# Two expert stages of a two-layer transformer: expert choice inside the stage, match-and-replace, sums by ScalarE, low weight parts by VectorE

## The chip, the cores and the metric

One core of a Trainium2 chip runs the whole program. The metric is the device time of one launch in microseconds (us); lower is better. The median of three launches is given for the kernel before; one further launch was profiled, and all rows of the trace are from that one.

## The reference

Two layers work on x, 2 sequences of 1024 tokens with 128 features (2048 tokens, 16 tiles of 128, 4 chunks of 512). Layer 0 is causal attention (16 heads of 64) and a mixture of 24 packed expert blocks. Layer 1 is a linear attention, and then a block with RMS norm, rotary attention (16 heads of 8), a gate and 8 experts of which each token takes one. What the change touches is, in short:

```python
# layer 0, choice and mixture (E=32, K=4, I=96: 32 x 96 columns are packed as 24 x 128)
scores = sigmoid(x @ gate_w.T)
_, ids = top_k(scores + e_bias, 4)
w = take(scores, ids); w = w / sum(w)
combine = zeros(T, 32).at[tokens, ids].add(w)
out = einsum(silu(x @ w1) * (x @ w3) * combine, w2)
# layer 1: RMS norm ahead of q, k, v
h = ln1_w * x * rsqrt(mean(x * x) + 1e-6)
# layer 1, choice and mixture (E=8, K=1, 256 hidden)
top1 = argmax(h2 @ Wr + br)
u1, u2 = split(h2 @ W1 + b1)
y = (u1 * sigmoid(u2)) @ W2 + b2, of expert top1 alone
```

## The kernel before

The program is a row of stages, each a block in which the five engines run their own lists and after which they meet at a barrier. In order: `stage_load`; `stage_ln` n0; `stage_attention64` a0; n1; `stage_combine` c0; `stage_experts` e0; n2; `stage_linear`; n3; `stage_rope`; `stage_attention8` a1; `stage_gate`; c1; e1; `stage_finish`. Every DMA is issued by SyncE (SP), so there is one queue.

**The choice** (`stage_combine`, L1108 to L1184) works on the logits of all 16 tiles. For layer 0 ScalarE takes the sigmoid (L1129) and VectorE adds the bias (L1144). VectorE finds each tile's eight largest (L1146), asks for their places (L1149), casts the places (L1151), compares them one rank at a time with a ramp 0..31 (L1155) and adds the masks (L1158); it multiplies by the scores, sums, inverts and scales (L1160 to L1163). TensorE transposes the 16 tiles (L1173), VectorE copies them out (L1167), and SP stores the table to DRAM (L1183; three copies for e0, since 32 experts of 96 columns lie in 24 blocks of 128). Layer 1 takes one expert, without scores.

**The experts** (`stage_experts`, L1187 to L1432). Values and weights are each split in a high part, rounded to the fast matmul format, and a low part, the rest; a product is three matmuls. A job is one chunk of 512 tokens with one 128-wide column block: e0 has 24 experts of 4 jobs, e1 8 experts of 8 jobs. For each job TensorE does six up matmuls (L1286) into two banks; ScalarE applies silu or sigmoid to one (L1359, L1361) and VectorE multiplies (L1416, L1418), which frees the banks; VectorE multiplies by the expert's row of the choice table (L1423), ScalarE rounds the product (L1339), VectorE takes the low part (L1397), and TensorE does three down matmuls (L1298) that accumulate in banks 4 to 7. TensorE runs two jobs ahead in the up part. On VectorE the order within job i is L1416 of job i, L1397 of job i-1, L1423 of job i.

The next expert's weights are rounded by ScalarE at its job 1 (L1329, up) and job 3 (L1333, down), and GpSimd subtracts to get the low parts (L1379). SP's order per expert is: wait until the low parts two experts earlier are taken; load the up weights (L1247, L1248) and down weights (L1251); wait until the expert before last is through (`f_full`); load the expert's rows of the table, broadcast over the partitions, as four DMAs of 256 KB (L1255). e1 has one DMA of 1 MB there, and starts with four bias matmuls that multiply the 8-row table (L1305).

**The norm with RMS** (`stage_ln` n3): TensorE transposes the centred tiles back (L192), ScalarE scales them out (L306) and squares them (L310), TensorE sums the squares by a matmul with a column of ones (L208) beside each tile's projection (L210), ScalarE takes the root of the four sums (L316), VectorE inverts (L263) and scales the tile (L1959).

## Time and profile before

| | |
|---|---|
| median of three launches | 1588.23 us (1587.38 to 1591.88) |
| profiled execution, whole | 1587.51 us |
| profiled execution, span of the trace | 1585.8 us |
| TensorE (PE) busy | 1323.0 us, 83% |
| VectorE (DVE) busy | 1019.7 us, 64% |
| ScalarE (ACT) busy | 666.4 us, 42% |
| GpSimd (POOL) busy | 206.5 us, 13% |
| mean granted TensorE clock | 0.893 |

In the rows, times count from the span's start; "idle before <-releaser" is how long the engine had stood still and what ended that. A group of several instructions stands as one row with its count (x4), and its second number is then the time from the first start to the last end. PEld are weight loads, SPq is the DMA issue on SyncE. A granted clock of 1.00 is 2.4 GHz, 0.50 is 1.2 GHz.

### The profile page before, as it was taken

To read this page: it belongs to the slowest core of one execution; us is meant where nothing else is said; L and a number is where in the kernel's file an instruction comes from. 1 tells how busy PE (TensorE), PEld (TensorE's weight loads), DVE (VectorE), ACT (ScalarE), POOL (GpSimd) and SP (SyncE) were. 2 spreads that over 40 slices of the span, in tenths; PEclk is the share of its full clock that TensorE was granted. 3 is DMA by queue.
4 is the path that set the end of the run, shared out by engine and by line. 5 is a ranking of instruction groups with operands and counts; after the bars stand their busy time and mean duration, and the time that the engine had idled before them with its cause. 6 is when DMAs were issued, how large, how long until landed. Compare 5 with 4: busy or idle time off the path is not lost. (4 is left out here: it accounts for less than half of the span.)

```text
span 1585.8 us, 19829 instructions
## 1 busy us (share of the span) xinstructions
PE 1323.0 (83%) x6224; PEld 806.0 (51%) x6224; DVE 1019.7 (64%) x1731; ACT 666.4 (42%) x1222; POOL 206.5 (13%) x417
## 2 busy tenths in 40 slices
PE   4789999999999999546999987614898988579997
PEld 3345555555655555234777765512343443146886
DVE  4645556475746462266999985564777875057998
ACT  2133434334243423134555555221366666215664
POOL 0001111111111111001111100031011111003110
PEclk9689999999999999768999998555799999568998
DMA  3110202111120201106676720034032211103220
GB/s 86 32 36 6 54 10 54 37 26 42 21 63 0 62 0 31 31 1 140 137 151 132 152 63 1 0 98 115 1 72 55 53 46 28 52 2 120 74 99 27
DMA packets 42833, 87.67 MB, mean 55 GB/s; under 512 B 13601, under 2 KB 31657, under 8 KB 37545
## 3 DMA queue, kind: packets, MB, share of 16 engines
q1 hardware_dynamic: 42768, 86.86, 23.0%
q8 instruction: 35, 0.57, 0.2%
q14 instruction: 30, 0.24, 0.0%
HBM read 69.47 MB, written 8.45 MB: 49 GB/s over the span
## 5 line engine op out<-in xcount | busy, mean ns | idle before, releaser
L646 ACT ACTIVATE shared<-ps 128x1024 f32<-128x1024 f32 (+7 forms) x256 | 165.9, 651 | 358.6 <-PE ps L495 358.0
L510 PE MATMUL ps<-shared,Vg 128*65 128x512 f32 (+3 forms) x768 | 291.1, 487 | 10.8 <-POOL shared L677 8.5
L1286 PE MATMUL ps<-qA 128*128 128x512 f32 x960 | 254.5, 401 | 19.2 <-DVE qA L1403 12.9
L561 DVE TENSOR_REDUCE mraw<-ps 128x1 f32<-128x512 f32 (+3 forms) x304 | 195.9, 659 | 89.4 <-PE ps L462 61.3
L964 DVE TENSOR_REDUCE mraw<-ps 128x2 f32<-128x1024 f32 (+3 forms) x160 | 174.0, 1114 | 76.5 <-PE ps L884 57.6
L1286 PEld LDWEIGHTS ps<-qA 128*128 128x128 f32 x960 | 178.3, 191 | 76.7 <-DVE shared L1416 18.1
L1008 ACT ACTIVATE shared<-ps 128x512 f32<-128x512 f32 (+2 forms) x320 | 154.2, 563 | 127.0 <-PE ps L900 126.8
L493 PE MATMUL ps<-qA,kH 128*128 128x512 f32 (+3 forms) x384 | 168.2, 446 | 2.6 <-DMA qB<-mT 2.6
L456 PE MATMUL ps<-kH,qA 128*128 128x512 f32 (+3 forms) x384 | 162.7, 464 | 6.2 <-DVE mraw L561 2.8
L510 PEld LDWEIGHTS ps<-shared,Vg 128*65 128x65 f32 x768 | 98.4, 138 | 118.4 <-issue 83.5
L1339 ACT CAST qA<-shared 128x512 fp32r<-128x512 f32 x160 | 99.3, 621 | 134.9 <-DVE shared L1423 134.5
L677 POOL TENSOR_SCALAR_AFFINE_SELECT shared<-shared 128x128 f32<-128x128 f32 x256 | 81.0, 317 | 526.4 <-ACT shared L646 526.4
L1298 PE MATMUL ps<-qA,kH 128*128 128x512 f32 x480 | 136.0, 392 | 4.3 <-DVE qA L1397 4.3
L495 PE MATMUL ps<-qB,kL 65*128 65x512 f32 (+3 forms) x384 | 134.4, 350 | 0.0
L1423 DVE TENSOR_TENSOR shared<-shared 128x512 f32<-128x512 f32 x160 | 132.3, 827 | 0.1
L1397 DVE TENSOR_TENSOR qA<-shared,qA 128x512 fp32r<-128x512 f32 x160 | 112.3, 702 | 10.9 <-ACT qA L1339 1.4
L1298 PEld LDWEIGHTS ps<-qA,kH 128*128 128x128 f32 x480 | 89.6, 188 | 25.5 <-DVE qA L1397 6.6
L456 PEld LDWEIGHTS ps<-kH,qA 128*128 128x128 f32 x384 | 72.4, 201 | 53.1 <-DVE mraw L561 30.3
L873 PE MATMUL ps<-kL,qA 64*128 64x512 f32 (+3 forms) x288 | 65.7, 436 | 36.1 <-DMA kH<-k_split 30.3
L900 PE MATMUL ps<-qA,kH 64*128 64x512 f32 (+3 forms) x288 | 81.5, 446 | 12.9 <-ACT shared L1008 8.1
L917 PE MATMUL ps<-shared,VP 128*32 128x512 f32 (+3 forms) x768 | 88.3, 536 | 0.5 <-ACT oU L996 0.5
L493 PEld LDWEIGHTS ps<-qA,kH 128*128 128x128 f32 x384 | 74.3, 193 | 27.3 <-issue 16.9
(227 smaller groups left out, 1595.9 us busy)
## 6 DMA issues: line engine op xcount, KB each, us to landing
shared<-comb SPq DMA_DIRECT2D x96, 256.0 KB, 4.5
qB<-qA SPq DMA_DIRECT2D x8, 1024.0 KB, 7.0
rB<-a0rec_dram SPq DMA_DIRECT2D x8, 1024.0 KB, 7.2
shared<-comb SPq DMA_DIRECT2D x8, 1024.0 KB, 4.4
q_split<-qA SPq DMA_DIRECT2D x8, 512.0 KB
qA<-q_split SPq DMA_DIRECT2D x16, 256.0 KB, 4.4
rB<-a1rec_dram SPq DMA_DIRECT2D x32, 128.0 KB, 2.7
e0wUp<-in_w SPq DMA_DIRECT2D x48, 64.0 KB, 4.6
```

Of the source, the lines that this page charges most:

```text
L456: ins = nc.tensor.matmul(bank[:, j * width:(j + 1) * width], k.qA[par][:, h0 + j, qt * P:(qt + 1) * P], k.kH[par][:, ch * 512:ch * 512 + w ...
L493: nc.tensor.matmul(region[:, lo:hi], kH[:, kt * P:(kt + 1) * P], qA[:, h, lo:hi], start=True, stop=False)
L495: ins = nc.tensor.matmul(region[:, lo:hi], kL[0:hd + 1, kt * P:(kt + 1) * P], qB[0:hd + 1, h, lo:hi], start=False, stop=True)
L510: ins = nc.tensor.matmul(O[0:65, lo:hi], k.Vg[par][:, kt, :], k.PT[:, slot % PTR, lo:hi], start=(kt == 0), stop=(kt == 4 * ch + 3))
L561: ins = nc.vector.tensor_reduce(out, bank[:, 0:n_h * width].rearrange("p (h w) -> p h w", w=width), AX, ALU.max)
L646: nc.scalar.activation(k.PT[:, slot % PTR, kt * P:S], score_banks(slot)[:, kt * P:S], ACT.Exp, scale=scale).then_inc(p_full, 1)
L964: nc.vector.tensor_reduce(out[:, :, js[0]:js[-1] + 1, qt % 4], src, AX, ALU.max).then_inc(x_free, 1)
L1008: nc.scalar.activation(dst, src, ACT.Exp, scale=scale).then_inc(p_done, 1)
L1286: ins = nc.tensor.matmul(bank[0:M, :], w[par][:, at:at + M], h[:, cols], start=(r == 0), stop=(r == 2))
L1298: ins = nc.tensor.matmul(acc(ch), w[par][:, m * D:(m + 1) * D], f[0:M, i % 2, :], start=(opens and r == 0), stop=(closing and r == 2), ski ...
L1397: nc.vector.tensor_tensor(fL[0:M, i % 2, :], k.hid[0:M, i % 2, :], fH[0:M, i % 2, :].bitcast(F32), ALU.subtract).then_inc(a_full, 1)
L1423: nc.vector.tensor_tensor(k.hid[0:M, i % 2, :], mul, k.cb[0:M, par, ch * 512:(ch + 1) * 512], ALU.mult).then_inc(f_full, 1)
```

## The change

It has six parts, and nothing else moves.

1. `stage_combine` is gone; its work stands at the head of `stage_experts`, so that weight loads, the splitting of values and weights, and the first up job run in the same block as the choice.
2. The choice uses match-and-replace: the unwanted ranks of the eight largest are overwritten, the tile's matching values are replaced by a mark, and a comparison with the mark gives the mask.
3. The rows of expert 0 come from a matmul of the table with a constant 0/1 matrix (`k.sel`) and not from DRAM. e0 reads them in PSUM, e1 has them copied by ScalarE.
4. The low parts of the weights are made by VectorE (GpSimd keeps those of expert 0), and ScalarE rounds the next up weights at job 0 and not at job 1.
5. In n3 the outputs are transposed once more, and ScalarE squares and sums in one instruction per tile; the matmuls with ones are gone.
6. The first two q/k weight loads of a0 are issued in `stage_load`.

```diff
+                for group in range(2):
+                    sp.dma_start(k.wqk[:, group, :], a["wqk0"][0]).then_inc(k.a0_in[group], 16)
                 for dst, src in later:
...
                 if rms:
-                    pe.wait_ge(squared, ch + 1)
+                    for t in range(4 * ch, 4 * ch + 4):
+                        ins = nc.tensor.transpose(k.bank(4 + ch)[:, (t % 4) * P:(t % 4 + 1) * P],
+                                                  dst[:, t * P:(t + 1) * P], k.ident[:, :])
+                    ins.then_inc(squared, 1)
...
-                    if rms:
-                        nc.tensor.matmul(k.bank(t % 4)[:, width:width + 1], sq[:, t * P:(t + 1) * P],
-                                         k.one_col[:, :], start=True, stop=True)
...
+                for t in range(4 * ch, 4 * ch + 4):
+                    ins = nc.scalar.activation(sq[:, t * P:(t + 1) * P], k.bank(4 + ch)[:, (t % 4) * P:(t % 4 + 1) * P],
+                                               ACT.Square, accum_out=k.rms_sum[:, t:t + 1])
+                ins.then_inc(summed, 1)
...
# stage_experts, SP
-                load(0, 0)
+                sp.wait_ge(copied, NC)
+                for r in range(copies):
+                    sp.dma_start(rows[:, r, :], k.cT[0:CE, :]).then_inc(stored, 16)
+                sp.wait_ge(stored, 16 * copies)
                 load(1, 1)
...
# TensorE
+                up(0, 0, 0)
+                pe.wait_ge(weights, 1)
+                for t in range(NT):
+                    ins = nc.tensor.transpose(acc(t // 4)[0:CE, (t % 4) * P:(t % 4 + 1) * P], comb[:, t, :],
+                                              k.ident[:, :])
+                for ch in range(NC):
+                    if ch == 1:
+                        up(0, 0, 1)
+                    pe.wait_ge(copied, ch + 1)
+                    nc.tensor.matmul(acc(ch), k.sel[0:CE, choose.sel, :], k.cT[0:CE, ch * 512:(ch + 1) * 512],
+                                     start=True, stop=True, skip_group_check=True).then_inc(rows_full, 1)
...
# ScalarE, per expert
-                        if i == 1 and not last:
+                        if i == 0 and not last:
                             split(e + 1, 1 - par, half + par)
...
# GpSimd
+                low(0, wL[0], wUp[:, 0, :], wH[0])
+                low(1, dL[0], wD[0:M, 0, :], dH[0])
-                with pool.Fori(0, E // 2) as j:
-                    for par in range(2):
-                        low(4 * j + 2 * par, wL[par], wUp[:, par, :], wH[par])
-                        low(4 * j + 2 * par + 1, dL[par], wD[0:M, par, :], dH[par])
...
# VectorE
+                low_part(0)
+                if choose.gated:
+                    link(nc.vector.tensor_tensor(logits[:, :, :], score[:, :, :],
+                                                 choose.e_bias.unsqueeze(1).broadcast_to((P, NT, CE)), ALU.add))
+                for t in range(NT):
+                    ins = nc.vector.max(top[:, t, :], logits[:, t, :])
+                link(nc.vector.memset(top[:, :, choose.K:8], ABSENT))
+                for t in range(NT):
+                    ins = nc.vector.match_replace(comb[:, t, :], top[:, t, :], logits[:, t, :], CHOSEN)
+                if choose.gated:
+                    link(nc.vector.scalar_tensor_tensor(out=comb[:, :, :], in0=comb[:, :, :], scalar=CHOSEN,
+                                                        in1=score[:, :, :], op0=ALU.is_equal, op1=ALU.mult))
+                    link(nc.vector.tensor_reduce(tot[:, 0, :], comb[:, :, :], AX, ALU.add))
+                    link(nc.vector.reciprocal(tot[:, 1, :], tot[:, 0, :]))
+                    nc.vector.tensor_tensor(comb[:, :, :], comb[:, :, :], column(tot[:, 1, :], NT, CE), ALU.mult)\
+                        .then_inc(weights, 1)
+                for ch in range(NC):
+                    if ch + 1 < NC:
+                        low_part(ch + 1)
+                    dve.wait_ge(turned, ch + 1)
+                    nc.vector.tensor_copy(k.cT[0:CE, ch * 512:(ch + 1) * 512], acc(ch)[0:CE, :]).then_inc(copied, 1)
...
+                        if i == 0 and not last:
+                            low_weights(2 * e + 2, wL[1 - par], wUp[:, 1 - par, :], wH[1 - par])
+                        if i == 3 and not last:
+                            low_weights(2 * e + 3, dL[1 - par], wD[0:M, 1 - par, :], dH[1 - par])
```

VectorE at job 0 of expert 1 in e0, up to the first step of job 1; `shared` holds the gate, the product and the rows of the table, `ps` the banks, `qA` the split parts. Before:

```order
L1416 TENSOR_TENSOR shared<-ps,shared 128x512 [waits e0s_full,e0ld1]
L1397 TENSOR_TENSOR qA<-shared,qA 128x512 [waits e0f_high]
L1423 TENSOR_TENSOR shared<-shared 128x512 [waits e0up_free]
L1416 TENSOR_TENSOR shared<-ps,shared 128x512 [waits e0s_full]
L1397 TENSOR_TENSOR qA<-shared,qA 128x512 [waits e0f_high]
```

Now, with the lines of the changed kernel (L1353 is the old L1397, L1429 the old L1423, L1373 the low parts of the weights):

```order
L1416 TENSOR_TENSOR shared<-ps,shared 128x512 [waits e0s_full,e0ld1]
L1353 TENSOR_TENSOR qA<-shared,qA 128x512 [waits e0f_high]
L1429 TENSOR_TENSOR shared<-shared 128x512 [waits e0up_free]
L1373 TENSOR_TENSOR qA<-e0wUp,qA 128x256 [waits e0w_high]
L1416 TENSOR_TENSOR shared<-ps,shared 128x512 [waits e0s_full]
L1353 TENSOR_TENSOR qA<-shared,qA 128x512 [waits e0f_high]
```

One instruction more stands behind the last step of job 0, and one (128x128) behind that of job 3.

TensorE at the head of the first expert stage. Before, in two blocks:

```order
L1173 MATMUL ps<-ident,c0comb 32x128 [waits c0weights]
L1173 MATMUL ps<-ident,c0comb 32x128 x15
L1125 UNCONDITIONAL_BRANCH
L1274 UNCONDITIONAL_BRANCH [waits barrier_Pool_Activation_PE_DVE_SP_release]
L1286 MATMUL ps<-qA 128x512 [waits e0up_free,e0w_low,e0h_low]
L1286 MATMUL ps<-qA 128x512 x5
L1286 MATMUL ps<-qA 128x512 [waits e0up_free]
```

Now, in one (L1227 the up matmuls, L1247 the transposes of the table, L1255 the 0/1 matmuls):

```order
L1227 MATMUL ps<-qA 128x512 [waits e0up_free,e0h_low,e0w_low]
L1227 MATMUL ps<-qA 128x512 x5
L1247 MATMUL ps<-ident,oU 32x128 [waits e0weights]
L1247 MATMUL ps<-ident,oU 32x128 x15
L1255 MATMUL ps<-y,sel 128x512 [waits e0copied]
L1227 MATMUL ps<-qA 128x512 [waits e0up_free,e0h_low]
L1227 MATMUL ps<-qA 128x512 x5
L1255 MATMUL ps<-y,sel 128x512 [waits e0copied] x3
```

The first up job now runs ahead of the transposes, and four fp32 matmuls over 512 columns are new.

## Rows read from the trace of the kernel before

**Rows 1.** Timeline, layer 0 from norm n1 to expert 1: start, duration, engine, line, out<-in.
```profile
699.12 1.59 DVE L1146 MAX8 c0top<-logits 128x8 f32<-128x32 f32 x16
...
703.44 0.23 DVE L1151 CAST c0atf<-c0at 128x128 f32<-128x128 uint32 x1
...
711.48 3.60 PE L1173 MATMUL ps<-ident,c0comb 128*32 128x128 f32 x16 [15.56 <-DVE c0pick L1164]
...
715.82 1.45 SPq L1183 DMA_DIRECT2D comb<-y  x3
721.36 0.36 SPq L1247 DMA_DIRECT2D e0wUp<-in_w  x1
...
739.96 0.68 DVE L1416 TENSOR_TENSOR shared<-ps,shared 128x512 f32<-128x512 f32 x1
```

**Rows 2.** Timeline, e0, end of one expert and the next one's start.
```profile
774.29 0.68 DVE L1423 TENSOR_TENSOR shared<-shared 128x512 f32<-128x512 f32 x1
...
775.00 0.62 ACT L1339 CAST qA<-shared 128x512 fp32r<-128x512 f32 x1 [0.86 <-DVE shared L1423]
...
775.65 0.69 DVE L1397 TENSOR_TENSOR qA<-shared,qA 128x512 fp32r<-128x512 f32 x1
...
776.18 0.77 POOL L1379 TENSOR_TENSOR qA<-e0wUp,qA 128x256 fp32r<-128x256 f32 x1 [3.74 <-ACT qA L1329]
776.26 1.23 DVE L1423 TENSOR_TENSOR shared<-shared 128x512 f32<-128x512 f32 x1
...
777.71 0.38 SPq L1248 DMA_DIRECT2D e0wUp<-in_w  x1
...
782.29 0.59 ACT L1359 ACTIVATE shared<-ps 128x512 f32<-128x512 f32 x1
```

**Rows 3.** Timeline, e0, VectorE's first step of the last expert.
```profile
932.10 0.68 DVE L1416 TENSOR_TENSOR shared<-ps,shared 128x512 f32<-128x512 f32 x1
```

**Rows 4.** Up weights of two experts, issue to landing, windows 777.2:778.1 and 786.2:787.1.
```profile
DMA to landing us min/median/max: 4.9/5.0/5.0
...
DMA to landing us min/median/max: 4.3/4.4/4.5
```

**Rows 5.** Groups by shape, VectorE, a 128x128 tensor_tensor.
```profile
L1155 DVE TENSOR_TENSOR c1comb<-iota,c1atf 128x128 f32<-128x128 f32 x1 | 0.3, 291 | 0.0
```

**Rows 6.** Timeline, e1, last experts, TensorE not held up.
```profile
1554.62 1.52 PE L1286 MATMUL ps<-qA 128*128 128x512 f32 x6
...
1562.78 1.52 PE L1286 MATMUL ps<-qA 128*128 128x512 f32 x6
```

**Rows 7.** Timeline, e1, the same ScalarE step four experts apart.
```profile
1474.61 0.62 ACT L1329 CAST qA<-e1wUp 128x512 fp32r<-128x512 f32 x1
...
1541.47 0.62 ACT L1329 CAST qA<-e1wUp 128x512 fp32r<-128x512 f32 x1
```

**Rows 8.** Timeline, norm n3: transposes back (chunks 2 and 3), two ScalarE tiles, last scaling.
```profile
1010.65 1.09 PE L192 MATMUL ps<-ident,oU 128*128 128x128 f32 x4 [1.40 <-ACT oU L298]
...
1016.20 0.87 ACT L298 ACTIVATE oU<-x_res,ln_nb,ln_rs 128x128 f32<-128x128 f32 x2
...
1017.21 1.09 PE L192 MATMUL ps<-ident,oU 128*128 128x128 f32 x4 [1.21 <-ACT oU L298]
...
1028.84 1.39 DVE L1959 SCALAR_TENSOR_TENSOR shared<-ps,rms_r,rows 128x192 f32<-128x192 f32 x4
```

**Rows 9.** Timeline, c1 and head of e1: search, bias matmuls, third up job.
```profile
1415.57 1.19 DVE L1146 MAX8 c1top<-logits 128x8 f32<-128x8 f32 x16 [0.30 <-PEq L1679]
...
1427.09 7.16 PE L1305 MATMUL ps<-y,b 8*128 8x512 f32 x8 [3.61 <-PEq L1125]
...
1441.20 1.66 PE L1286 MATMUL ps<-qA 128*128 128x512 f32 x6 [1.26 <-DVE shared L1418]
```

**Rows 10.** Windows, head of e1: PE, PEld, DVE, ACT, POOL busy, PEclk, DMA.
```profile
1430.00:1433.00 3.00, 3.00 (x4) 1.11 (x4) 1.81 (x3) 2.71 (x6) 3.00 (x3) 0.50 0.95 295
```

**Rows 11.** Timeline, head of a0.
```profile
42.01 5.54 PE L446 MATMUL ps<-hT,wqk 128*128 128x512 f32 x8 [3.25 <-DMA wqk<-in_wqk]
```

More of the change, by code:

```diff
@@ L30 @@
 MASKED = -1e30
+ABSENT = -3e38
+CHOSEN = 3e38
 LN_EPS, RMS_EPS = 1e-5, 1e-6
@@ L1211, in stage_experts @@
         JOBS = NC * MT
-        parts = comb_dram.shape[0] // E
+        parts = 4 if choose.gated else 1
         NLD = 16 * (parts + (bias is not None))
+        CE, logits = choose.E, choose.logits
+        scored, weights, turned, copied, stored, rows_full, rows_taken, links = (
+            sem(n) for n in ("scored", "weights", "turned", "copied", "stored", "rows_full", "rows_taken", "links"))
+        score, comb = (k.oU_flat[:, i * NT * CE:(i + 1) * NT * CE].rearrange("p (t e) -> p t e", t=NT)
+                       for i in range(2))
+        top = sb("top", [P, NT, 8])
+        tot = sb("tot", [P, 2, NT])
         UP = 2 * MT * M
@@ L1263, in _ @@
                     load_down(e, e)
-                load(0, 0)
+                if bias is not None:
+                    sp.dma_start(bi[:, 0, :], one(bias, 0)).then_inc(ld[0], 16)
+                sp.wait_ge(copied, NC)
+                copies = comb_dram.shape[0] // CE
+                rows = comb_dram.rearrange("(e r) t -> e r t", r=copies)
+                for r in range(copies):
+                    sp.dma_start(rows[:, r, :], k.cT[0:CE, :]).then_inc(stored, 16)
+                sp.wait_ge(stored, 16 * copies)
                 load(1, 1)
@@ L1345, in _ @@
                     nc.scalar.copy(hH[:, cols], hT[:, cols]).then_inc(h_high, 1)
+                    if ch == 0 and choose.gated:
+                        nc.scalar.activation(score[:, :, :], logits[:, :, :], ACT.Sigmoid).then_inc(scored, 1)
+                    if ch == 0:
+                        split(0, 0, 0)
+                        split_down(0, 0, 0)
+                if MT > 1:
+                    for ch in range(NC):
+                        act.wait_ge(rows_full, ch + 1)
+                        nc.scalar.copy(k.cb[:, 0, ch * 512:(ch + 1) * 512], acc(ch)).then_inc(rows_taken, 1)
                 def expert(e, par, half, first=False, last=False):
                     if bias is not None:
-                        act.wait_ge(ld[par], NLD * (half + 1))
+                        act.wait_ge(ld[par], NLD * (half + 1) if par else NLD * half + 16)
                     for i in range(JOBS):
@@ L1406, in expert @@
+                for ch in range(NC):
+                    if ch + 1 < NC:
+                        low_part(ch + 1)
+                    dve.wait_ge(turned, ch + 1)
+                    nc.vector.tensor_copy(k.cT[0:CE, ch * 512:(ch + 1) * 512], acc(ch)[0:CE, :]).then_inc(copied, 1)
                 def expert(e, par, half, first=False, last=False):
-                    dve.wait_ge(ld[par], NLD * (half + 1))
+                    if not first:
+                        dve.wait_ge(ld[par], NLD * (half + 1) if par else NLD * half + 16 * (bias is not None))
+                    elif bias is not None:
+                        dve.wait_ge(ld[0], 16)
```

163 lines of the change are left out of this document (58 added, 105 removed).

## The prediction

> **What bounds the kernel now.** The busy shares (TensorE 83%, VectorE 64%) are means over fifteen stages, so I read the timeline of each stage that the change touches, then the windows for the granted clock, and last the landing times of the weight loads. The attention stages are left alone but for one load.
>
> At the head of e0 TensorE stands still for long stretches, since choice, table, loads and splitting come one after the other: VectorE starts the search at 699.12, the transposes start at 711.48, the stores at 715.82, the first weight load only at 721.36, and expert 1 starts on VectorE at 739.96 [rows 1].
>
> Inside e0 a ring of VectorE and ScalarE sets the pace, not a sum of busy times. L1423 starts at 774.29; its result is rounded by ScalarE from 775.00 for 0.62; L1397 starts at 775.65 and the next L1423 at 776.26 [rows 2]. That is 1.97 us per job. VectorE has three steps in it that follow each other at 0.61 (775.65 to 776.26), so 0.14 is free. Where GpSimd makes low parts at the same time, L1423 takes 1.23 and not 0.68 [rows 2]. Over experts 1 to 22 the period is (932.10 - 739.96) / 22 = 8.73 us [rows 1, 3], against 4 x 1.97 = 7.88 for the bare ring. So GpSimd's company costs 0.85 per expert. TensorE, where nothing holds it up, needs (1562.78 - 1554.62) / 4 = 2.04 us per job [rows 6], 8.16 per expert. It is the next floor.
>
> **The change, part by part**, against the profiled execution (1587.51 us; its span is 1585.8, so 1.7 lie around it, and it is 0.7 below the median of the three runs).
>
> *First loads of a0.* TensorE waits 3.25 us for them [rows 11]. With them issued in the first stage the wait goes. What is left is the start of the block, some tenths. Gain 2.0 to 3.2, taken **2.5**.
>
> *Head of e0, data path.* The new search starts about 0.6 after the old one, since VectorE takes a low part first: 699.7. Sixteen searches take 1.6 [rows 1], to 701.3. A memset and sixteen match-and-replace follow: the nearest rows are the sixteen index finds, from 700.7 to 703.44, 2.7 us [rows 1]; the bounds are 1.6 (one instruction each, as the search) and 4. That gives 704.1. Four steps then stand for twelve: mask times score, sum, scale at 0.7 each and a reciprocal, 2.5 in all: 706.6, against 711.48 before. Transposes 3.6 [rows 1]: 710.2. Four copies of 0.68 alternate with low parts of 0.6, so the last ends at 711.6. The stores take 721.36 - 715.82 = 5.5 from first issue to next load, a little less without the barrier, 5.2: 716.8. Then come the rows and weights of the next experts. In steady state the second up load is issued at 777.71, which is 2.74 after L1423 ended at 774.97, and lands 4.4 to 5.0 later [rows 2, 4], so 7.1 to 7.7 after the burst begins, taken 7.5: 724.3. Rounding those weights and the first gate cost 1.0, since both now stand ahead of expert 1's first step: 725.3, against 739.96. Gain 14.7.
>
> *Head of e0, TensorE's path.* The 0/1 matmuls are fp32 over 512 columns, as the bias matmuls of e1, of which four chunks took 7.16 at 1.2 GHz [rows 9, 10]; between half of that and the whole. The up job before the second of them costs 1.4 to 2.6. From 710.2, all at 1.2 GHz, job 2's matmuls would end at 722.3 and expert 1 start at 727.0: gain 13. At 2.4 GHz the data path decides. I take **14**, with 12 to 15.5 as bounds.
>
> *Steady e0.* GpSimd's 0.85 goes. VectorE takes the low parts instead: 128x256 and 128x128. A 128x128 one lasts 0.29 [rows 5], 512 wide 0.69, so 256 wide 0.42 between them. Followers overlap by 0.08, so they occupy 0.34 and 0.21. Less the 0.14 that is free each time, the ring grows to 7.88 + 0.20 + 0.07 = 8.15, level with TensorE's 8.16. But the up weights are now rounded at job 0 instead of job 1, **ahead of a gate that the ring needs**. The load is issued behind the 1 MB of rows and lands 7.1 to 7.7 after the expert before last ended. Rounding 256 columns delays the gate by some 0.3 (512 take 0.62 [rows 2]), and ScalarE starts 0.05 after a landing. The gate takes 0.59 [rows 2], and L1416 may come 0.12 after the end of the last L1423, behind the new low part, which starts 0.08 before that end and occupies 0.2; so the gate must start 0.5 before that end if the ring is to stay whole. The period is at least 7.1 to 7.7 plus 0.3 + 0.05 + 0.5, or 7.95 to 8.55, and over TensorE's 8.16 on average 8.37. Before, the rounding came one job later and found the weights there. Gain (8.73 - 8.37) x 22 = **8**, between 0 and 12.5. GpSimd's own work is not needed elsewhere in that stage. SP's wait for low parts is met earlier than its wait for `f_full`, so its loads move with the experts and no further.
>
> *n3.* One cycle is 1017.21 - 1010.65 = 6.56, the tail 1028.84 + 1.39 - 1017.21 = 13.0 [rows 8]. TensorE loses the matmuls with ones and gains four transposes per chunk (1.09, rows 8). The important part is that ScalarE no longer waits for the projections before it takes the root and then the next centring. The new squares are unseen in this trace: between 0.2 and 0.65 each, the nearest row being two tiles of 128x128 in 0.87 [rows 8], taken 0.4. A cycle is then a transpose back and a transpose (2.1), four squares (1.6), the root and centring (1.3): 5.0. Over one and a half cycles and a shorter tail the gain is 3.5 to 8.8, taken **5.5**.
>
> *Head of e1.* The block now starts with the search, at 1415.6 [rows 9]. Load, rounding and GpSimd's low part take some 4.7 (2.7, 0.6 and 1.4, as estimates), so the first up job ends near 1422.9, and the transposes, 3.6 as in e0 [rows 1], near 1426.5. There the bias matmuls could start, 0.6 before now; but the four 0/1 matmuls (3.6 to 7.2) and the second up job (1.4 to 2.6) now stand ahead of them. The bias matmuls ran from 1427.09 for 7.16 us without a gap, and the granted clock in 1430 to 1433 was still 0.50, 1.2 GHz [rows 9, 10]. Eight-row matmuls do not raise it here. All at 1.2 GHz the third up job ends at 1426.5 + 7.2 + 2.6 + 7.2 + 2.6 = 1446, against 1442.9 now [rows 9]; with the up jobs at 2.4 GHz near 1441; all at 2.4 GHz near 1436.5. Gain -3 to +6.5, taken **2**. The Trainium skill, page "TensorE: Matmul & The Clock Gate", Part 1, says that "the default state is throttled, and activity releases the throttle". Read plainly, a TensorE that is busy throughout would run this head at the high level, for a gain of 6.5. The trace speaks against it for eight-row matmuls.
>
> *Steady e1.* The period is (1541.47 - 1474.61) / 4 = 16.72 [rows 7]. Ring 8 x 1.98, plus low parts of twice the width less the free time, 0.69: 16.53, over TensorE's 16.32. Gain 0.19 x 7 = **1.3**, between 0 and 2.8.
>
> Sum: 2.5 + 14 + 8 + 5.5 + 2 + 1.3 = 33.3. 1587.5 - 33.3 = **1554 us**.
>
> **Rivals.**
> A. *The weights land in time anyway.* The two landings differ by 0.6 [rows 4], and at the early end the period is 8.16, so e0 gains 12.6 and the time is 1549.5. The late landing speaks against it. Chance 0.25.
> B. *The steady part gives nothing*: each expert waits 0.4 longer than forecast for weights, and the period stays 8.73. 1562. Chance 0.17.
> C. *The clock is high in both heads.* e1 gains 6.5 and e0 15: 1549. The clock in rows 10 speaks against it. By the page's rule above this would be the course. Chance 0.10.
> D. *Slower: ScalarE's early rounding turns every expert into a DMA round trip.* ScalarE's queue holds gate and rounding of the product behind the wait, so every microsecond of a late landing is one of the ring. The other terms give 25.3. To be slower by 0.3% the period must reach 8.73 + (25.3 + 4.8) / 22 = 10.1, a landing 9.3 after the burst begins. At 10.2 the time is 1594.5. For it: the 1 MB stands ahead of the weights in SP's queue. Against: the landings seen are 7.1 to 7.7. Chance 0.05, of which 0.02 end within 0.3%.
>
> **How the numbers follow.** The forecast has 0.43, A 0.25, B 0.17, C 0.10, D 0.05. A measurement of this kernel can tell about 0.3% (4.8 us) from no change. All but D are faster by more: faster 0.95, same 0.02, slower 0.03. The low end takes A and C together with a good n3 (1554 - 4.6 - 5 - 3 = 1541), the high end B with a head of e1 at 1.2 GHz and little from n3 (1554 + 8 + 5 + 1 = 1568).
>
> **What would show it.** Right: the first up load issued within 1 us of the stage's start; stores some 4 us earlier than before; expert 1 of e0 starting 14 us earlier after the last logits; L1429 at 0.68 throughout; an e0 period near 8.4 with ScalarE's L1281 waiting for the DMA of `wUp`; TensorE idle before the third up job of e1. Wrong: a period of 8.16 with no such wait (A) or 8.7 (B); a granted clock of 1.00 during the bias matmuls (C); n3 cycles still over 6 us, if a square with its sum costs more than 0.65.

## The result

| | before | changed |
|---|---|---|
| median, us | 1588.93 (1587.38 to 1591.88, 4 runs) | 1547.91 (1539.19 to 1555.47, 4 runs) |
| ratio, 95% interval | | 0.9737 (0.9694 to 0.978) |
| profiled execution, its span | 1587.51, 1585.8 | 1549.17, 1547.5 |

The kernel is 2.6% faster, 41 us by the medians; 1554 was forecast, with 1541 to 1568 as the range. I divide the 38.3 us between the two profiled executions by steps that both traces have. The last column is the same changed kernel profiled once more (experiment 9); its gains sum to 48.1.

| stretch | before | changed | gain | forecast | gain, second profile |
|---|---|---|---|---|---|
| start to the last logits of e0 | 696.15 | 694.24 | 1.9 | 2.5 | 1.9 |
| to expert 1 of e0 (its first step on VectorE) | 43.81 | 32.56 | 11.25 | 14 | 14.3 |
| expert 1 to 23 of e0 | 192.14 | 181.49 | 10.65 | 8 | 11.3 |
| to the first step of n3 | 62.18 | 64.08 | -1.9 | 0 | -0.9 |
| n3 | 35.95 | 24.14 | 11.8 | 5.5 | 11.6 |
| attention and gate of layer 1 (unchanged) | 385.04 | 385.67 | -0.6 | 0 | 4.8 |
| gate's end to expert 1 of e1 | 41.86 | 38.95 | 2.9 | 2 | 2.8 |
| expert 1 to 7 of e1 | 100.30 | 99.18 | 1.1 | 1.1 | 1.1 |
| expert 7 to the end | 28.37 | 27.19 | 1.2 | 0.2 | 1.2 |

### The profile after

Timeline of the head of e0, which answers to [rows 1]. L1179 is a load of up weights, L1381 the search, L1392 the last step of the choice, L1247 the table's transposes, L1202 the stores, L1255 the 0/1 matmuls, L1187 the rows of expert 1, L1227 the up matmuls, L1416 VectorE's first step of a job.

```profile
694.51 0.33 SPq L1179 DMA_DIRECT2D e0wUp<-in_w  x1
...
697.85 1.59 DVE L1381 MAX8 e0top<-logits 128x8 f32<-128x32 f32 x16
...
704.10 0.69 DVE L1392 TENSOR_TENSOR oU<-oU,e0tot 128x512 f32<-128x512 f32 x1
...
704.85 3.59 PE L1247 MATMUL ps<-ident,oU 128*32 128x128 f32 x16 [3.47 <-DVE oU L1392]
708.37 2.07 PE L1255 MATMUL ps<-y,sel 32*128 32x512 f32 x2
...
709.62 1.45 SPq L1202 DMA_DIRECT2D comb<-y  x3
710.37 2.93 PE L1227 MATMUL ps<-qA 128*128 128x512 f32 x6
713.23 5.49 PE L1255 MATMUL ps<-y,sel 32*128 32x512 f32 x6
...
714.77 1.72 SPq L1187 DMA_DIRECT2D shared<-comb  x4
...
718.65 5.05 PE L1227 MATMUL ps<-qA 128*128 128x512 f32 x12
...
726.80 0.69 DVE L1416 TENSOR_TENSOR shared<-ps,shared 128x512 f32<-128x512 f32 x1
```

From 704.85 on TensorE has no gap up to expert 1: it is the engine that the head waits for. The windows (busy times, then the granted clock, where 1.00 is 2.4 GHz) say at which level it ran:

```profile
698.00:715.00 17.00, 13.08 (x32) 7.19 (x33) 13.47 (x65) 4.78 (x8) 0.82 (x2) 0.50 0.23 50
715.00:727.00 12.00, 12.00 (x33) 7.70 (x32) 5.12 (x10) 3.68 (x8) 0.00 (x0) 0.66 0.50 105
```

Inside e0: groups from 727 to 908 (busy, mean ns, idle before and its cause), and one expert's end in the timeline, which answers to [rows 2].

```profile
L1429 DVE TENSOR_TENSOR shared<-shared 128x512 f32<-128x512 f32 x88 | 60.1, 683 | 0.0
...
L1281 ACT CAST qA<-e0wUp 128x256 fp32r<-128x256 f32 x21 | 8.5, 407 | 12.3 <-DMA e0wUp<-in_w 12.3
```

```profile
776.29 1.87 SPq L1187 DMA_DIRECT2D shared<-comb  x4
...
783.55 0.68 DVE L1429 TENSOR_TENSOR shared<-shared 128x512 f32<-128x512 f32 x1
783.75 0.41 ACT L1281 CAST qA<-e0wUp 128x256 fp32r<-128x256 f32 x1 [0.84 <-DMA e0wUp<-in_w]
784.07 0.59 ACT L1318 ACTIVATE shared<-ps 128x512 f32<-128x512 f32 x1
...
784.69 0.69 DVE L1416 TENSOR_TENSOR shared<-ps,shared 128x512 f32<-128x512 f32 x1 [0.25 <-ACT shared L1318]
...
908.29 0.68 DVE L1416 TENSOR_TENSOR shared<-ps,shared 128x512 f32<-128x512 f32 x1
```

L1429 (the old L1423) takes 0.68 to 0.69 everywhere. ScalarE's rounding, which waited for the weights, starts 7.46 us after SP's burst of loads began (776.29 to 783.75), inside the forecast's 7.1 to 7.7. ScalarE's gate starts 0.32 later, and VectorE waits 0.25 for it. The mean period is (908.29 - 726.80) / 22 = 8.25, against 8.73 in [rows 1, 3].

Timeline of n3, which answers to [rows 8]: L196 turns back, L208 are the new transposes, L214 the projections, L317 the squares with the reading of their sum. The first row is from the kernel before: ScalarE's root, which waited 2.83 us for TensorE's projections; the squares now wait 1.25 for the transposes alone.

```profile
1016.04 0.26 ACT L316 ACTIVATE rms_std<-ps,eps 128x4 f32<-128x4 f32 x1 [2.83 <-PE ps L210]
```

```profile
985.57 0.77 PE L196 MATMUL ps<-ident,oU 128*128 128x128 f32 x4
...
986.17 0.60 PE L208 MATMUL ps<-ident,hT 128*128 128x128 f32 x4
...
986.61 1.47 PE L214 MATMUL ps<-ffn_w,hT 128*128 128x192 f32 x8
987.05 0.27 ACT L317 ACTIVATE rB<-ps 128x128 f32<-128x128 f32 x1
987.21 0.20 ACT L317 ACTIVATION_READ_ACCUMULATOR rB<-ps 128x1 f32 x1
987.30 0.27 ACT L317 ACTIVATE rB<-ps 128x128 f32<-128x128 f32 x1
...
989.43 0.63 PE L196 MATMUL ps<-ident,oU 128*128 128x128 f32 x4 [1.35 <-ACT oU L302]
...
990.53 0.28 ACT L317 ACTIVATE rB<-ps 128x128 f32<-128x128 f32 x1 [1.25 <-PE ps L208]
...
995.12 1.39 DVE L1975 SCALAR_TENSOR_TENSOR shared<-ps,rms_r,rows 128x192 f32<-128x192 f32 x4
```

This cycle is 3.86 (985.57 to 989.43) against 6.56, and the tail from the last turn back 7.1 against 13.0. From about 986 on TensorE runs at the high level (granted clock 0.96 from 985 to 997): four transposes take 0.60 to 0.63, against 1.09 in [rows 8]. The cycle before it still ran at the low level (0.50 from 981 to 985, transposes of 1.08 and 1.06) and took 4.55, so most of the shorter cycle was there without the high clock.

Timeline of the head of e1, which answers to [rows 9]:

```profile
1392.75 1.12 PE L1255 MATMUL ps<-y,sel 8*128 8x512 f32 x2
...
1395.39 2.84 PE L1255 MATMUL ps<-y,sel 8*128 8x512 f32 x6
...
1398.07 6.22 PE L1260 MATMUL ps<-y,b 8*128 8x512 f32 x8
```

The first 0/1 matmul takes 1.12 for its two records, where the first one of e0 took 2.07, and the other three take 2.84; the granted clock from 1390 to 1398 is 0.87. The bias matmuls (L1260) took 6.22, 0.9 less than in [rows 9].

### The profile page after: what moved, and what is told of

It reads as the page before. It is cut to its first block and busy times, and to the rows that moved or that the text cites. A ratio compares the mean times of both kernels' runs of the same rounds, so it can differ in the third digit from the quotient of the medians.

```text
span 1547.5 us, 19708 instructions
## 1 busy us (share of the span) xinstructions
PE 1316.2 (85%) x6224; PEld 806.3 (52%) x6224; DVE 1002.8 (65%) x1782; ACT 678.9 (44%) x1254; POOL 157.7 (10%) x357
## 5 line engine op out<-in xcount | busy, mean ns | idle before, releaser
L516 PE MATMUL ps<-shared,Vg 128*65 128x512 f32 (+3 forms) x768 | 291.0, 487 | 11.3 <-POOL shared L683 8.5
L1227 PE MATMUL ps<-qA 128*128 128x512 f32 x960 | 254.3, 402 | 10.1 <-POOL qA L1337 10.1
L1227 PEld LDWEIGHTS ps<-qA 128*128 128x128 f32 x960 | 183.1, 194 | 60.6 <-POOL qA L1337 11.8
L1291 ACT CAST qA<-shared 128x512 fp32r<-128x512 f32 x160 | 99.2, 620 | 90.9 <-DVE shared L1429 90.1
L1353 DVE TENSOR_TENSOR qA<-shared,qA 128x512 fp32r<-128x512 f32 x160 | 109.9, 687 | 6.4 <-ACT qA L1291 1.4
L1429 DVE TENSOR_TENSOR shared<-shared 128x512 f32<-128x512 f32 x156 | 106.6, 683 | 0.0
```

Source lines behind the costliest of these rows:

```text
L516: ins = nc.tensor.matmul(O[0:65, lo:hi], k.Vg[par][:, kt, :], k.PT[:, slot % PTR, lo:hi], start=(kt == 0), stop=(kt == 4 * ch + 3))
L1227: ins = nc.tensor.matmul(bank[0:M, :], w[par][:, at:at + M], h[:, cols], start=(r == 0), stop=(r == 2))
L1353: nc.vector.tensor_tensor(fL[0:M, i % 2, :], k.hid[0:M, i % 2, :], fH[0:M, i % 2, :].bitcast(F32), ALU.subtract).then_inc(a_full, 1)
L1429: nc.vector.tensor_tensor(k.hid[0:M, i % 2, :], mul, rows, ALU.mult).then_inc(f_full, 1)
```

## The experiments

The edits are to the kernel before (1, 2, 6, 11) or to the changed one. Spans of stretches are those of the table. Ratios are to runs of the kernel before on the same chip.

**1. `b_n3`: the kernel before with the new n3 alone.** The edit is the diff of the change in `stage_ln`, with the sums kept in `k.rms_r` until the reciprocals take their place.

> The kernel before with the new n3 alone (squares with their sums by ScalarE, over transposes back). The trace of the changed kernel says that n3 gave 11.8 us, not the 5.5 forecast. Theory 1 (n3 stands by itself): from the first step of n3 on VectorE to the end of the last scaling 24 to 25 us against 35.95 before, transposes back 3.9 us apart, and a time of 1588.9 - 11.8 = 1577 us. Theory 2 (part of what n3 showed came from the state in which the earlier stages left TensorE's clock or from other parts): n3 takes 28 to 31 us and the time is near 1583. Both: L208's transposes let TensorE's projections run at the higher clock, 1.5 us for eight and not 2.8.

Measured: 1579.97 us, ratio 0.9942 (0.9913 to 0.997), 9.2 us less. The first and last VectorE steps of n3:

```profile
995.97 0.32 DVE L270 TENSOR_SCALAR ffn_w<-ffn_w,cols 128x192 f32<-128x192 f32 x1 [0.31 <-PEq L1454]
...
1018.78 1.39 DVE L1961 SCALAR_TENSOR_TENSOR shared<-ps,rms_r,rows 128x192 f32<-128x192 f32 x4
```

n3 takes 24.2 us and stands by itself: theory 1. The gain of the whole kernel, 4.8 to 13.8 by the interval, is compatible with 11.8.

**2. `b_turns`: more transposes in the old n3.**

```
                 if rms:
+                    for t in range(4 * ch, 4 * ch + 4):
+                        nc.tensor.transpose(k.bank(4 + ch)[...], dst[...], k.ident[:, :])
                     pe.wait_ge(squared, ch + 1)
```

> The kernel before, with four transposes per chunk more on TensorE in n3, whose results nobody uses; squares and sums stay as they were. If the higher granted clock is what made n3 short (the transposes keep TensorE busy, the projections then run at 2.4 GHz), n3 shrinks from 35.95 to 30 to 33 us though TensorE has more to do. If it is the chain (ScalarE no longer waits for projections before root and next centring), n3 grows to 37 to 40 us here, 0.5 to 1.1 us per chunk for the transposes, with cycles of 6.5 to 7.5 us.

Measured: 1599.01, one run; n3 takes 38.05, 2.1 more than before. The turns back of chunks 2 and 3:

```profile
1015.90 1.09 PE L192 MATMUL ps<-ident,oU 128*128 128x128 f32 x4 [1.40 <-ACT oU L301]
...
1023.32 1.09 PE L192 MATMUL ps<-ident,oU 128*128 128x128 f32 x4 [1.21 <-ACT oU L301]
```

The cycle grows from 6.56 to 7.42 and the clock stays at 0.50 from 1009 to 1036. More work for TensorE is not what shortened n3, and did not bring the high clock; the chain is the theory left.

**3. `a_pool`: low parts of the weights by GpSimd again,** rounding left at job 0.

```
...
+                with pool.Fori(1, E // 2) as j:
+                    for par in range(2):
+                        low(4 * j + 2 * par, wL[par], wUp[:, par, :], wH[par])
+                        low(4 * j + 2 * par + 1, dL[par], wD[0:M, par, :], dH[par])
...
-                        if i == 0 and not last:
-                            low_weights(2 * e + 2, wL[1 - par], wUp[:, 1 - par, :], wH[1 - par])
...
```

> The changed kernel with the low parts of the weights made by GpSimd again, from expert 1 on; the rounding stays at job 0. If GpSimd's company is what cost 0.85 per expert (L1429 at 1.23 us where both run), the period of e0 grows from 8.25 to 8.7 to 9.0 us and the time by 10 to 16 us over the changed kernel, so 1558 to 1564. If the landing of the weights sets the period now, GpSimd's part overlaps with slack: the period stays within 8.25 to 8.35 and the time within 1546 to 1550.

Measured: 1546.44, ratio 0.971 (0.9653 to 0.9767), experts 1 to 23 of e0 in 179.8, a period of 8.17. The first theory falls as it was put: GpSimd's company costs nothing here. The second, that GpSimd's part overlaps with slack, is nearer, but 8.17 lies below its 8.25 to 8.35. In e1, experts 1 to 7 take 97.4, against 99.2 in the changed kernel: there GpSimd's low parts are the cheaper ones. Timeline of one low part:

```profile
780.89 0.81 POOL L1337 TENSOR_TENSOR qA<-e0wUp,qA 128x256 fp32r<-128x256 f32 x1 [1.50 <-ACT qA L1281]
...
781.34 0.69 DVE L1422 TENSOR_TENSOR shared<-ps,shared 128x512 f32<-128x512 f32 x1 [0.25 <-ACT shared L1318]
```

The VectorE step that starts inside GpSimd's span is one with an operand in PSUM, and keeps its 0.69. From 745 to 900 that is so 38 times, at 0.69 on average. In the trace of before it was the product with the rows, both operands in SBUF, in all 36 cases of the same window, at 1.09 on average (0.95 or 1.23, as in [rows 2]). The Trainium skill, page "SBUF — State Buffer", section "SBUF: two separate sides", says the same: a VectorE instruction "in a 2-port perf mode, or with two SBUF inputs" and a GpSimd one that reads SBUF exclude each other, and the one that starts second waits. By that rule, the trace agrees.

**4. `a_split1`: rounding and low part of the up weights back at job 1,** still by VectorE.

```
-                        if i == 0 and not last:
+                        if i == 1 and not last:
                             split(e + 1, 1 - par, half + par)
...
```

> The changed kernel with the rounding of the next up weights (and their low part) back at job 1. If the wait of ScalarE's L1281 for the weights is what keeps the period at 8.25 and not 8.16, it goes: no idle before L1281 for the DMA in e0, period 8.16 to 8.18, 2 us less over 22 experts, about 1546. If the order of steps around the low part costs instead, the period stays at 8.25 or grows to 8.4 since TensorE waits for the low part of the weights at the next expert's first job.

Measured: 1545.57, ratio 0.971 (0.9655 to 0.9765). The period is (903.23 - 723.52) / 22 = 8.17, TensorE's 8.16 in nearly every expert, and the wait for the DMA is gone. Group of L1281, 727 to 908:

```profile
L1281 ACT CAST qA<-e0wUp 128x256 fp32r<-128x256 f32 x21 | 8.5, 407 | 11.7 <-PE ps L1227 11.7
```

So the early rounding costs the changed kernel 0.08 per expert, 1.8 us in all (0.05 against the second profile, experiment 9): the forecast's mechanism, at less than half its size (8.37 - 8.16 = 0.21).

**5. `a_order`: SP asks for weights ahead of rows.**

```
...
+                        load_weights(2 * j + par + 1, 1 - par)
                         sp.wait_ge(f_full, JOBS * (2 * j + par - 1))
                         load(2 * j + par, par)
...
```

> The changed kernel with SP's queue in another order: the weights of expert e+1 are asked for ahead of the 1 MB of rows of expert e, not behind it. If ScalarE's wait at job 0 is for weights that queue behind the rows, it goes: no idle before L1281 for the DMA, period of e0 8.16, gain 2 us (1546). If it is the landing time by itself, or if rows now come late for VectorE's L1429, the period is 8.25 or more.

Measured: 1547.86, ratio 0.9784 (0.9741 to 0.9827). The wait for weights went, and another came: the period is 8.43. Group of VectorE's first step of a job, 727 to 900:

```profile
L1424 DVE TENSOR_TENSOR shared<-ps,shared 128x512 f32<-128x512 f32 x83 | 56.9, 686 | 5.8 <-DMA shared<-comb 5.6 <-issue 0.2
```

The rows, now last in the queue, come late for VectorE. Whichever of the two loads is asked for last comes late for its first user. Experiment 4 moved that user by a job for the weights; nothing of the kind was tried for the rows.

**6. `b_split0`: the kernel before with the rounding at job 0.** One line, `i == 1` to `i == 0`.

> The kernel before with one thing changed: ScalarE rounds the next expert's up weights at job 0, not job 1, so GpSimd's low part of them starts elsewhere against VectorE's steps. The run with GpSimd's low parts in the changed kernel had L1429 at 0.69 throughout, and GpSimd beside a step that reads PSUM. Theory 1 (the 0.55 came only because GpSimd's work began just ahead of a VectorE step with both operands in SBUF): the period of e0 falls from 8.73 to 8.16 to 8.3, L1423 at 1.23 goes, about 10 us less: 1578. Theory 2 (GpSimd's company costs the ring whatever its moment; in the other run something else, the shorter queue or the table's place, made room): period 8.6 to 8.8 and no change of time.

Measured: 1581.24, ratio 0.9965 (0.9931 to 0.9998). Experts 1 to 23 of e0 take 183.8 (8.36 each) and not 192.1; L1423 is at 1.23 in 2 experts and not in 22, but the down weights' low part still meets it at 0.95, 23 times. Theory 1, at 8.3 us and not 10, and with a period just above its 8.16 to 8.3. The line also acts in e1, which the expectation left out: experts 1 to 7 take 97.4 and not 100.3, 2.9 less. Against that, expert 1 starts 1.4 later in e0 and 1.3 later in e1. One line of the change gives four fifths of what e0's steady part gained, and in e1 more than the changed kernel (1.1); 5.6 us arrive in the kernel's time (0.3 to 11).

**7. `a_warm`: unused transposes at the heads,** on top of the edit of 5.

```
...
+                keep_busy(13)
                 up(0, 0, 0)
+                keep_busy(12)
                 pe.wait_ge(weights, 1)
```

> As the run before, with 13 transposes of 128x128 whose results nobody uses ahead of the first up job and 12 behind it in both expert stages, in time in which TensorE stands still. Theory 1 (the heads are long because TensorE starts them at 1.2 GHz out of idle time): the transposes of the table, 3.6 us now, and the 0/1 matmuls, 0.85 to 1 each now, run at 2.4 GHz (1.9 in all and 0.48 each); expert 1 of e0 starts 24 to 28 us after the last logits and not 32.8; 5 to 9 us less in all, about 1540. Theory 2 (narrow matmuls with 32 or 8 rows keep or bring the lower clock whatever went before): the table's transposes may be short, but the 0/1 and bias matmuls are at 1.2 GHz again; gain 0 to 3 us.

Measured: 1546.89, ratio 0.9747 (0.9704 to 0.9789). The head of e0, TensorE (L1254 the unused ones, L1262 the table's, L1270 the 0/1 matmuls):

```profile
699.17 1.86 PE L1254 MATMUL ps<-ident,hT 128*128 128x128 f32 x12
702.83 1.92 PE L1262 MATMUL ps<-ident,oU 128*32 128x128 f32 x16 [1.81 <-DVE oU L1407]
704.68 1.12 PE L1270 MATMUL ps<-y,sel 32*128 32x512 f32 x2
...
707.33 2.84 PE L1270 MATMUL ps<-y,sel 32*128 32x512 f32 x6
```

All narrow matmuls of this head run faster: 1.92 for 3.59, and 1.12 + 2.84 for 2.07 + 5.49. Expert 1 starts 26.9 us after the last logits, 2.6 sooner than in experiment 5 (29.5), to which this run adds the transposes. Of the 5.6 us to the changed kernel's 32.6, 3.1 are there without them. Theory 1 holds for the matmuls that it names: from 702 to 710 the granted clock is 1.00, so matmuls of 32 rows run at the high level when TensorE comes to them busy. But behind them it fell again, though TensorE had no gap:

```profile
710.20:713.60 3.40, 3.40 (x8) 2.67 (x9) 0.41 (x1) 0.60 (x2) 0.00 (x0) 0.50 0.53 116
```

`a_again` has the same: 1.00 from 714 to 716, under the 0/1 matmuls, and 0.50 from 717 to 720, behind them. So theory 2 is not out; whether the narrow matmuls bring the clock down is not shown, since no run fills their place with wide ones. In e1 nothing came (39.7 from the gate's end to expert 1, against 38.95). In the whole kernel it can't be told from experiment 5, whose interval overlaps with this one's.

**8. `a_rowsdma`: rows of expert 0 of e0 by DMA as before,** its four 0/1 matmuls left out.

```
+                if MT == 1:
+                    load(0, 0)
                 load(1, 1)
```

> The changed kernel, where in e0 the rows of expert 0 come by DMA from the stored table as before, and the four 0/1 matmuls of e0 are gone (e1 is left as it is). If those matmuls are what held the head (7.6 us of them at 1.2 GHz on TensorE's path), the rows land about 5 us after their issue, at 720 where L1429 took the matmul's at 711, but expert 1 starts only 0 to 3 us later than in the changed kernel. If the DMA round trip is what the 0/1 matmuls save, expert 1 starts 5 to 8 us later (732 to 735 on the same scale).

Measured: 1554.18, one run; expert 1 starts 35.6 us after the last logits, 3.1 later than in the profile of the changed kernel and 6.1 later than in its repeat. VectorE stood still for 11.7 us until the rows had landed, and TensorE as long:

```profile
719.75 0.69 DVE L1432 TENSOR_TENSOR shared<-shared 128x512 f32<-128x512 f32 x1 [11.71 <-DMA shared<-comb]
```

The 0/1 matmuls are worth 3 to 6 us, by the level that they meet; neither theory's numbers alone.

**9. `a_again`: the changed kernel, nothing altered.**

> The changed kernel once more, with nothing altered. Its times lie between 1539 and 1555 us and the profiles of its variants disagree on stages that no variant touches: from the end of n3 to the end of the last gate 380.5 to 396.8 us. Theory 1 (the granted clock of TensorE differs from one execution to the next at the same instructions): expert 1 of e0 starts either 29.4 or 32.6 us after the last logits with the same instructions, n3 24.1 to 24.7, e0 from expert 1 to 23 again 181 to 182, and the stretch without changes anywhere in 378 to 397. Theory 2 (the first profile is typical, the differences come from the edits): 32.6, 181.5 and 385.7 again, within 0.5.

Measured: 1540.66 (1532.31 to 1548.86, 4 runs), ratio 0.9677 (0.9606 to 0.9749). The same instructions as in the timeline above, from the table's 0/1 matmuls on:

```profile
713.26 2.92 PE L1255 MATMUL ps<-y,sel 32*128 32x512 f32 x6
...
723.81 0.69 DVE L1416 TENSOR_TENSOR shared<-ps,shared 128x512 f32<-128x512 f32 x1
```

Expert 1 starts 29.55 us after the last logits and not 32.56: L1255 takes 2.92 for 5.49. `a_split1`, `a_pool` and `a_order` also have 29.3 to 29.6, and `a_ones`, whose edit lies in n3, has 32.0. The unchanged stretch took 380.25. Over all profiles of this study it took 378.5 to 396.8. Windows of it, first of `b_n3` (378.5 in all), then of `a_pool` (396.8):

```profile
1220.00:1320.00 100.00, 88.58 (x784) 39.94 (x776) 76.36 (x82) 66.33 (x139) 15.86 (x26) 1.00 0.19 45
1320.00:1398.70 78.70, 53.59 (x297) 25.66 (x289) 22.11 (x40) 30.83 (x61) 6.97 (x11) 0.78 0.11 32
```

```profile
1190.00:1290.00 100.00, 89.37 (x740) 40.55 (x738) 72.12 (x79) 63.87 (x133) 15.29 (x24) 0.92 0.20 49
1290.00:1387.00 97.00, 72.70 (x357) 33.41 (x349) 28.54 (x46) 36.83 (x73) 7.64 (x12) 0.70 0.10 27
```

Where the granted clock (the third column from the right) is lower, fewer instructions fit into the same 100 us. Theory 1 (though e0's 180.8 is just under its 181 to 182): the times of one kernel spread by 16 us for a cause outside the change. This kernel's median alone moved from 1547.91 to 1540.66 between the two sets of four runs. Terms of a few us can here be read from a stage alone.

**10. `a_ones`: one-column matmuls back in the new n3,** results unused.

```
+                    if rms:
+                        nc.tensor.matmul(k.bank(t % 4)[:, width:width + 1], dst[...],
+                                         k.one_col[:, :], start=True, stop=True)
```

> The changed kernel with the 16 one-column matmuls of the old n3 put back into TensorE's stream (chunks 1 to 3, results unused); ScalarE does not wait for them. Twelve of them at about 0.2 us are 2.4 us of TensorE time, half of it beside other work. Theory 1 (one-column matmuls keep the granted clock at its lower level, and their going let n3 run at the higher one): the projections of chunks 1 to 3 take 0.99 per two again and the clock of the stretch is 0.50; n3 takes 28 to 31 us against 24.1. Theory 2 (TensorE is at the higher level because it no longer stands idle between chunks, whatever the width): projections at 1.5 us for eight, n3 24.5 to 26.

Measured: 1548.90, one run; n3 takes 26.2, 2.0 more. Windows of it:

```profile
976.00:984.00 8.00, 8.00 (x36) 7.91 (x34) 3.87 (x18) 4.82 (x21) 0.00 (x0) 0.50 0.01 2
984.00:992.00 8.00, 7.70 (x57) 7.11 (x55) 4.03 (x14) 4.88 (x25) 0.00 (x0) 1.00 0.00 0
```

The clock rose to its high level at 984 with the one-column matmuls in the stream, after 8.8 us in which TensorE had no gap (from 975.17). Theory 1 falls; theory 2 fits, 0.2 beyond its range. It is not whole either: in `b_turns` TensorE was busy from 1023.32 to the end of its last matmul of n3 at 1035.2, but for 0.26, and stayed at 0.50.

**11. `b_choice`: the kernel before with the choice by match-and-replace alone.**

```
...
-                    ins = nc.vector.max_index(at[:, t, :], top[:, t, :], ranked[:, t, :])
+                    ins = nc.vector.match_replace(comb[:, t, :], top[:, t, :], ranked[:, t, :], CHOSEN)
...
```

> The kernel before with the choice by match-and-replace alone; stages, stores and rows as they were. In the changed kernel the steps from the first search to the weights took 6.4 us (697.85 to 704.3) against 12.4 before (699.12 to 711.48). If the choice is a chain that everything waits for, the stores come 5.5 to 6.5 us earlier after the last logits and expert 1 of e0 starts 37.5 to 38.5 us after them, not 43.8. If the first weights or TensorE's state take its place (TensorE goes into the transposes after a shorter rest), less than 4 us arrive at expert 1. In c1 the choice has few steps: 1 to 2 us.

Measured: 1583.43, one run. Expert 1 of e0 starts 39.0 us after the last logits, 4.8 earlier. The transposes start 10.2 after them, where it was 15.3 (711.48 in [rows 1], with the last logits at 696.15), so 5.2 earlier:

```profile
706.55 3.60 PE L1174 MATMUL ps<-ident,c0comb 128*32 128x128 f32 x16 [10.40 <-DVE c0pick L1165]
```

Search to transposes takes 7.2 here against 12.4 before. So 5.2 are gained there, and 4.8 of them arrive at expert 1: the chain theory, a little short of its numbers. (The expectation's 6.4 for the changed kernel was misread; its trace has 7.0, from 697.85 to 704.85.) From the gate's end to expert 1 of e1: 42.1 against 41.9, nothing.

**12. `a_best1`: what seemed best, together.** The edit of 3, the unused transposes of 7 in e0 only (without the order of 5), and in e1 the table and the 0/1 matrix in fp32r.

> The changed kernel with what the runs so far point to: low parts of the weights by GpSimd with the rounding at job 0 (e0 8.17 per expert, e1 16.24 instead of 16.53); 25 unused transposes in TensorE's rests at the head of e0 only; in e1 the table in fp32r, whose 0 and 1 are exact there, so that the 0/1 matmuls need one pass and not four. Theory 1 (the three add up): expert 1 of e0 27 us after the last logits (32.6 or 29.4 without), e0 179.8 from expert 1 to 23, head of e1 2 us shorter (37 from the gate's end to expert 1), e1 97.4 for six experts; 5 to 8 us less than the changed kernel in the mean. Theory 2 (the heads wait for DMA or VectorE once TensorE is faster): heads 29 and 38.5, gain 2 to 4 us, not to be told from the spread.

Measured: 1541.94, ratio 0.9678 (0.9623 to 0.9733), the same as `a_again` beside it. The head of e1 gave 3.8 where 2 was hoped: 35.25 for 39.05, with a first 0/1 matmul of 0.49 us and three more in 0.96, and with bias matmuls that here ran in 3.67, for 6.03 in `a_again`. The steady part of e1 gave what was hoped (97.4 for 99.2). But in e0 the period is 8.35. GpSimd's low parts (L1356) met the product with the rows again:

```profile
735.63 0.77 POOL L1356 TENSOR_TENSOR kH<-e0wD,kH 128x128 fp32r<-128x128 f32 x1 [5.44 <-ACT kH L1302]
736.00 0.95 DVE L1455 TENSOR_TENSOR shared<-shared 128x512 f32<-128x512 f32 x1
```

From 745 to 900 this product starts inside GpSimd's span 21 times, at 0.97 on average (18 times beside the down weights' low part, at 0.95). In e0 this kernel differs from `a_pool` only in its head, but each of the two was profiled once: whether the head or the execution decides where GpSimd falls is not shown. And expert 1 starts 29.2 us after the last logits, not 27: TensorE was done, but ScalarE waited for the weights of expert 2. They are asked for at 715.50, behind the table's stores and the rows; in `a_warm`, which had 26.9, the order of experiment 5 asks for them at 696.83.

```profile
721.08 0.40 ACT L1298 CAST qA<-e0wUp 128x256 fp32r<-128x256 f32 x1 [3.68 <-DMA e0wUp<-in_w]
```

Theory 1 holds for e1 and fails for e0. No version here is shown to be faster than the changed kernel.

## Why the prediction was right, and where it was off

**Sum and sign.** 33.3 forecast, 38.3 in the profiled execution. n3 gave 6.3 more than forecast and e0's steady part 2.65 more; e0's head gave 2.75 less, and the two untouched stretches cost 2.5. That the sum came within 5 us is in part luck: these misses partly cancel, the attention stretch alone was 4.8 shorter in the second profile than before, and the repeat's median (1540.66) lies just below the range's 1541.

**First loads of a0**: 2.5 forecast. TensorE starts at 39.89 and not 42.01 [rows 11]; 1.9 is left at the last logits, a little under the lower bound of 2.0. Over all profiles the last logits end at 696.2 to 699.8 in the five kernels with the old loads and at 692.1 to 694.6 in the nine with the new ones. Right.

**Head of e0**: 14 forecast, 11.25 and 14.3 found. TensorE's path is the one that decided in both profiles, as its gapless row shows: 13 in the forecast for 1.2 GHz throughout, 11.25 on the chip, and 14.3 where the clock rose earlier. The data path shows itself once TensorE is out of the way: 29.2 us from the last logits in `a_best1`, where the step had 43.8 - 14.7 = 29.1. The data path was priced rightly. TensorE's path came out 1.7 longer than its 13 allowed: the four 0/1 matmuls took 7.56 (2.07 + 5.49) for 7.16 and an up job 2.93 for 2.6, and the forecast's own terms add up to 722.6 for job 2 and not to its 722.3. That one kernel would differ by 3 us here from one execution to the next was not foreseen. The choice is worth 4.8 of it (`b_choice`), the matmul in place of the round trip 3 to 6 (`a_rowsdma`). The merged stage's share was not tried by itself.

**Steady e0**: 8 forecast, 10.65 found. "GpSimd's 0.85 goes" holds for the changed kernel: no product with the rows takes longer than 0.69. The rounding ahead of the gate does wait for the DMA, but cost 0.08 per expert and not 0.21. The landing was priced rightly (7.46 after the burst). What was mis-sized is the mean. The forecast's bounds of 7.95 and 8.55, taken evenly and with 8.16 as the floor, have 8.29 as their mean; it took 8.37, about the middle between floor and upper bound. In the trace some landings are late enough to cost and others not, and the expert after a late one often takes 8.11, less than the floor. Rival A's 8.16 is what `a_split1` shows. The reason given for the gain was incomplete: it is less who makes the low part than what VectorE starts meanwhile. `b_split0` gets 8.3 us with GpSimd left in place.

**n3**: 5.5 forecast with 3.5 to 8.8 as bounds, 11.8 found, outside them. This is the term that failed, by its size. From the start to the second turn back 1.0 is gained, in the two cycles after it 4.9 (981.02 to 989.43 now, 1003.90 to 1017.21 before), in the tail 5.9. Three things were mis-sized. A square with its sum follows the one before after 0.25 and was taken as 0.4: 0.6 per cycle. The two sets of transposes were priced at [rows 8]'s 2.1, at 1.2 GHz; in the cycle from 985.57 to 989.43 they take 1.5 to the first square, at the high clock: 0.6 more. And the tail, 7.1 where 13.0 was, got no number of its own in the forecast; two cycles and a tail that shrink by as much as they did don't fit into "one and a half cycles and a shorter tail". At the low level the last projections alone would add 1.3 to it (2.77 as in chunk 0, not 1.47). The mechanism, ScalarE freed from the projections, fits: its wait of 2.83 for them is gone in the trace, and `b_n3` shows that the new n3 gives the whole gain by itself. The matmuls with ones, which went with it, were not taken out alone; put back, they cost 2.0 (`a_ones`). The added transposes did not bring the high clock (`b_turns`), nor did the one-column matmuls hold it down (`a_ones`); that it follows from the missing stalls is the reading left, and it is not shown.

**Head of e1**: 2 forecast, 2.9 found, between the clock cases of -3 and 6.5: the clock was at 0.87 from 1390 to 1398 and at 0.57 during the bias matmuls, from 1398 to 1404. The forecast's "eight-row matmuls do not raise it" was read from the bias matmuls alone. The eight-row 0/1 matmuls ran at the high level (2.84 for three), but behind them, under the bias matmuls, the clock fell with TensorE busy, as it did in e0 behind the 0/1 matmuls of `a_warm` and `a_again`. So a TensorE busy throughout did not keep the high level, and in e0 it did not reach it from 704.85 to 718.65. Rival C came half true. The sign "TensorE idle before the third up job" did not come: the job starts as the bias matmuls end.

**Steady e1**: 0.19 per expert forecast and found. But with GpSimd's low parts and the rounding at job 0 the period is 16.24 (`a_pool`, `b_split0`) and not 16.53: here the move to VectorE costs 1.8 us over six experts.

**Rivals**: A had 12.6 for steady e0 and 1549.5 in all. Its sign, no wait for the weights, did not come, but its numbers are nearer to the measured 8.25, 10.65 and 1547.91 than the forecast's 8.37, 8 and 1554. B (8.73 kept) and D (a round trip in every period) did not come. D failed for the reason given against it: the weights are there 7.46 us after the burst began.

## What to carry to other kernels

Before moving work off GpSimd, look at which VectorE step starts beside it: shifting a rounding by one job gave most of the gain of moving the work. Where GpSimd's part falls, however, differed between `a_pool` and `a_best1`. With the work on VectorE no step was disturbed, at a price of 0.3 us per expert in e1. When a change shortens TensorE's stalls, price its matmuls at both levels of the clock. Where the granted clock spreads a kernel's time by 1%, compare stages between steps that both traces have, and profile the unchanged kernel twice.

## What was not expected of the hardware

- The same instructions ran at different granted clocks in two executions: six 0/1 matmul records took 5.49 us in one and 2.92 in the other, and an unchanged stretch 378.5 to 396.8 us.
- ScalarE's square with its sum is two instructions, 0.27 and 0.20, which follow each other so closely that the next square starts 0.25 after the first.
- A VectorE step with an operand in PSUM ran at 0.69 beside GpSimd, 38 times of 38 (`a_pool`); one with both in SBUF, started beside it, at 0.95 or 1.23, 36 times of 36 (before).
- TensorE, busy without a gap from 704.85, ran the last 0/1 matmuls at 1.2 GHz still, up to 718.65; 25 unused transposes in the rests before put the table's transposes and the 0/1 matmuls at 2.4 GHz, and behind these the clock was 0.50 again from 710.2 to 713.6, without a gap. What exactly raises the clock stays open.
